# An attention and mixture-of-experts layer on one core: another order of the steps at pass boundaries and in the first pass

## The reference, cut to what matters

```python
q = layernorm(x); k = v = ctx
ig, fg = gates(concat(q, k, v))
cs = cumsum(log_sigmoid(fg))
log_D = where(tril, cs[:, :, None] - cs[:, None, :], -inf) + ig[:, None, :]
D = exp(log_D - max(log_D))
C = (q @ k.T / sqrt(32)) * D
h = (C / (max(|C.sum()|, exp(-max(log_D))) + 1e-6)) @ v
x = x + layernorm(h) * ln_scale
u = layernorm(x)
h_s = sum over 2 shared experts of gelu(rmsnorm(u) @ W1 + b1) @ W2 + b2
h_r = sum over the top 2 of 8 routed experts, weighted by their gates
out = x + u + h_s + h_r
```

## Time and profile before

| what | us |
|---|---|
| median of 3 runs | 1325.37 (1324.14 to 1329.71) |
| the profiled execution's own time | 1325.87 |
| its span, first to last instruction | 1324.1 |
| PE busy | 1160.5 |
| DVE busy | 941.8 |
| ACT busy | 805.9 |
| unit 0 of batch 0 starts | 92.0 |
| pass 0 ends (base sum of batch 0) | 229.9 |
| steady passes | 91.8 to 95.7 each |
| the block of the routed tiles begins | 850 |

### The profile page before, as it was taken

One profiled execution on the slowest core, in us unless ns is written; L12 is line 12 of the kernel. 1 busy time (PEld: TensorE's weight loads), 2 busy tenths in 40 slices (PEclk: granted clock), 3 DMA queues, 4 the chain that ended last, 5 costly groups with the idle time before them and its releaser, 6 DMA issues. The chain is left out here.

```text
span 1324.1 us, 21782 instructions
## 1 busy us (share of the span) xinstructions
PE 1160.5 (88%) x7861; PEld 1016.8 (77%) x7861; DVE 941.8 (71%) x2263; ACT 805.9 (61%) x1392; POOL 348.4 (26%) x319
## 2 busy tenths in 40 slices
PE   2839984898998997997997979799999999999996
PEld 1537763677676775885875867799999999999996
DVE  6765659677686686595694545488888888888883
ACT  3315532554554564453564425399999999999994
POOL 7102132041131221221320202023333333333333
PEclk8859885999998998998998989899999999999998
DMA  5000000110010010010000103578888888888882
GB/s 184 32 17 17 16 33 32 32 64 33 19 47 33 29 37 32 33 33 32 33 17 17 41 1 113 160 228 236 232 219 219 223 234 237 236 226 221 219 223 25
DMA packets 141690, 136.16 MB, mean 103 GB/s; under 512 B 48598, under 2 KB 127584, under 8 KB 141584
## 3 DMA queue, kind: packets, MB, share of 16 engines
q1 hardware_dynamic: 122948, 111.68, 26.7%
q0 software_dynamic: 14304, 18.75, 8.5%
q10 hardware_dynamic: 4332, 4.34, 0.9%
HBM read 109.42 MB, written 25.33 MB: 102 GB/s over the span
## 5 line engine op out<-in xcount | busy, mean ns | idle before, releaser
L1328 DVE TENSOR_TENSOR wlo<-big,whi 128x512 fp32r<-128x512 f32 x312 | 220.1, 717 | 21.5 <-ACT whi L1281 14.3
L569 ACT ACTIVATE shared_hraw<-bank,b1s 128x512 f32<-128x512 f32 x128 | 88.0, 688 | 196.4 <-PE bank L1091 196.2
L1281 ACT CAST whi<-big 128x512 fp32r<-128x512 f32 x312 | 191.1, 615 | 5.4 <-PEq L414 5.1
L1253 PE MATMUL bank<-xhi,whi 128*128 128x256 f32 x624 | 175.7, 282 | 6.7 <-DVE xlo L1342 5.1
L1231 PE MATMUL bank<-whi,hhi 128*128 128x256 f32 x624 | 178.3, 286 | 0.0
L1231 PE MATMUL bank<-whi,hlo 128*128 128x256 f32 x624 | 174.6, 280 | 0.0
L1253 PE MATMUL bank<-xlo,whi 128*128 128x256 f32 x624 | 174.6, 280 | 0.0
L1231 PE MATMUL bank<-wlo,hhi 128*128 128x256 f32 x624 | 174.6, 280 | 0.0
L1253 PE MATMUL bank<-xhi,wlo 128*128 128x256 f32 x624 | 174.6, 280 | 0.0
L1074 PE MATMUL bank<-whs,shared_hhi 128*128 128x256 f32 x512 | 150.0, 293 | 27.4 <-DVE shared_hlo L811 27.4
L811 DVE TENSOR_TENSOR shared_hlo<-shared_hraw,shared_hhi 128x512 fp32r<-128x512 f32 x128 | 89.3, 703 | 117.1 <-ACT shared_hhi L572 115.1
(11 more groups left out here) (274 smaller groups left out, 2691.6 us busy)
## 6 DMA issues: line engine op xcount, KB each, us to landing
big<-in_L_ffn_W_r_dram SPq DMA_DIRECT2D x78, 1024.0 KB, 7.2
qcT<-sorted_tokens SPq DMA_DIRECT2D x39, 260.0 KB, 2.9
xb<-in_x_dram SPq DMA_DIRECT2D x8, 512.0 KB, 4.5
cb<-in_ctx_dram SPq DMA_DIRECT2D x8, 512.0 KB, 3.6
xr<-in_x_dram SPq DMA_DIRECT2D x8, 512.0 KB, 3.6
out_dram<-base ACTq DMA_DIRECT2D x8, 512.0 KB, 2.9
sorted_tokens<-chunk SPq DMA_DIRECT2D x9, 260.0 KB
out_dram<-yt,token POOLq DMA_INDIRECT x78, 4.0
```

Source lines behind the costliest of these rows:

```text
L569: nc.scalar.activation(hraw[:, k % NHB, :], up_bank[k % 2][:, :], ACT.Gelu, bias=b1s[:, k // M, k % M:k % M + 1]).then_inc(gelu_done, 1)
L1253: last = nc.tensor.matmul(ub[:, 0:T], w[i][:, wsl], x_[i][:, k, :], start=k == 0 and t == 0, stop=k == KD - 1 and t == 2)
L1281: nc.scalar.copy(whi[i][:, psl], raw[i][:, psl]).then_inc(t_whi, 1)
L1328: nc.vector.tensor_tensor(wlo[i][:, psl], raw[i][:, psl], whi[i][:, psl].bitcast(fp32), ALU.subtract).then_inc(t_wlo, 1)
```

## The change

Three things change.

The strings: in `START`, which ran only batch 0's `front` and `back`, the eight `g` steps of batch 1 now stand between the last rounds, the normalisation and the first two units of batch 0. `FIRST` opens with `S 0` and has its units between the steps of the attention of batch 1, as `ORDER` has. In all strings `A` (routing) moves behind the first `1`. The query mask of DVE becomes a step `M` of its own behind `G`. The last step of `front` is cut in two on DVE, `C` and `c`, at L715 and L716, and `c` comes behind the last unit of the pass.

The end of a pass: PE's last down projection (`late`, step `L`) moves behind the next pass's states and first scores. `finish` becomes the step `Y` behind `H`. The down banks' first write of a pass waits for `fin_ready`.

The waits and loads: PE's transposes of batch 1 wait for three blocks of batch 0 only, and no more for its logits. The load of batch 1's context moves ahead of the wait for the weight pieces.

```diff
--- before.py
+++ after.py
@@ -347,10 +347,10 @@
 
 
 
-        START = "f f f w w w f f w w f S w w w 0 w w 0 w w 1 w w 1 w 2 w 2 3 3 T T T V V V W h u X u".split()
-        FIRST = "g g U U g U U g U g U U U g U U S 0 U 0 A 1 U 1 Q F 2 U F 2 B P 3 U 3 D G T E T T R V V V R W X C".split()
-        ORDER = "S 0 H 0 U A 1 U F 1 U Q 2 U F 2 B U P 3 U 3 D U G T E U T U Z T U Z R V U V U V U R U W U X C U".split()
-        ORDER_6 = "S 0 H 0 U A 1 U 1 U Q 2 U 2 B U P 3 U 3 D U T E U T T U V U V V U W U X U U U U".split()
+        START = "f f f f w w w f f w w f f S w w w 0 w w 0 w w 1 w w g 1 w 2 w g 2 3 3 g T T T V V g g V W h g u g u X g".split()
+        FIRST = "S 0 U 0 1 A U 1 F U Q 2 U F 2 B U P 3 U 3 D G M T E U T U T R V U V U V U R U W U X C U c".split()
+        ORDER = "S 0 L H Y 0 U 1 A U 1 F U Q 2 U F 2 B U P 3 U 3 D U G M T E U T U Z T U Z R V U V U V U R U W U X C U c".split()
+        ORDER_6 = "S 0 L H Y 0 U 1 A U 1 U Q 2 U 2 B U P 3 U 3 D U T E U T T U V U V V U W U X U U U U".split()
         assert ORDER.count("U") == U and ORDER_6.count("U") == U and FIRST.count("U") + START.count("u") == U and START.count("w") == PIECES
         att_bank, up_bank, down_bank = psum[0:4], psum[4:6], psum[6:8]
 
@@ -377,6 +377,10 @@
                         k += 1
                     elif step == "H":
                         parts["hand_over"](b)
+                    elif step == "L":
+                        parts["late"](b - 1)
+                    elif step == "Y":
+                        parts["finish"](b - 1)
                     elif step == "P":
                         parts["base"](b)
                     elif step in "AQBDE" or step == "Z" and b == B - 1:
@@ -385,7 +389,7 @@
                         next(routes[b])
                     elif step == "d":
                         parts["idle"]()
-                    elif step in "FGRCfg":
+                    elif step in "FGMRCcfg":
                         f = 0 if step == "f" else 1 if step == "g" else b + 2
                         if f < B:
                             if f not in fronts:
@@ -395,8 +399,8 @@
                         if b + 1 not in backs:
                             backs[b + 1] = parts["back"](b + 1)
                         next(backs[b + 1])
-                if b >= 0:
-                    parts["finish"](b)
+            parts["late"](B - 1)
+            parts["finish"](B - 1)
 
         class Steps:
 
@@ -434,14 +438,16 @@
                 load(xb, x_v, 1, s_x)
                 sp.wait_ge(s_wls, 1)
                 sp.dma_start(slots_w[PIECES - 1], w_piece(PIECES - 1)).then_inc(s_wlast, 16)
+                sp.wait_ge(state_done, 1)
+                load(cb, c_v, 1, s_c)
                 sp.wait_ge(s_wls, PIECES - 1)
                 load(xr, x_v, 0, s_xr)
                 for b in range(1, B):
                     if b > 1:
                         sp.wait_ge(q_ready, b)
                         load(xb, x_v, b, s_x)
-                    sp.wait_ge(state_done, b)
-                    load(cb, c_v, b, s_c)
+                        sp.wait_ge(state_done, b)
+                        load(cb, c_v, b, s_c)
                     sp.wait_ge(x1_ready, b)
                     load(xr, x_v, b, s_xr)
                 sp.wait_ge(s_zero, 1)
@@ -521,6 +527,7 @@
                         nc.scalar.copy(qcT[:, :, j * P:(j + 1) * P],
                                        att_bank[j][:, :].rearrange("p (k s) -> p k s", s=P)).then_inc(qcT_ready, 1)
                     yield
+                    yield
                     sc.wait_ge(gates_done, b + 1)
                     if b == 0:
                         sc.wait_ge(s_gate, 16 * GATE_LOADS)
@@ -608,7 +616,7 @@
                     nc.scalar.copy(xhs[:, :, :], unT[:, :, :]).then_inc(xhs_ready, 1)
 
                 passes(sc, {"front": front, "back": back, "unit": unit, "hand_over": hand_over, "split": split, "idle": lambda: None,
-                            "base": lambda b: None, "finish": finish, "route": route})
+                            "base": lambda b: None, "finish": finish, "late": lambda b: None, "route": route})
 
             @block.vector
             def _(dve):
@@ -944,7 +954,7 @@
                     dve.sem_inc(tables_known, 1)
 
                 passes(dve, {"front": front, "back": back, "unit": unit, "hand_over": hand_over, "split": split, "idle": lambda: None,
-                             "base": to_add, "finish": finish, "route": route})
+                             "base": to_add, "finish": finish, "late": lambda b: None, "route": route})
 
             @block.tensor
             def _(pe):
@@ -956,11 +966,10 @@
 
                     pe.wait_ge(q_ready, b + 1)
                     pe.wait_ge(s_c, 16 * b + 16)
-                    if b > 0:
+                    if b == 1:
+                        pe.wait_ge(hn_ready, J - 1)
+                    if b > 1:
                         pe.wait_ge(hn_ready, J * b)
-                    if b == 1:
-                        pe.wait_ge(logit_read, 1)
-                    if b > 1:
                         pe.wait_ge(gT_ready, b - 1)
                     for j in range(J):
                         for k in range(KD):
@@ -1067,6 +1078,8 @@
                 def second(b, k):
 
                     pe.wait_ge(hlo_ready, U * b + k + 1)
+                    if b > 0 and k == 0:
+                        pe.wait_ge(fin_ready, b)
                     e, m = k // M, k % M
                     wsl = slice(WN + m * D, WN + (m + 1) * D)
                     for j in range(J):
@@ -1094,8 +1107,10 @@
                     if k >= LAG:
                         second(b, k - LAG)
                     if k == U - 1:
-                        for late in range(U - LAG, U):
-                            second(b, late)
+                        second(b, U - 2)
+
+                def late(b):
+                    second(b, U - 1)
 
                 def route(b):
                     yield
@@ -1139,7 +1154,7 @@
                     mm(psum[5][:, :], ident[:, :], ident[:, :].unsqueeze(1).to_broadcast([P, HG, P]), start=True, stop=True)
 
                 passes(pe, {"split": lambda n: None, "idle": idle, "front": front, "back": back, "unit": unit, "hand_over": lambda b: None,
-                            "base": lambda b: None, "finish": lambda b: None, "route": route})
+                            "base": lambda b: None, "finish": lambda b: None, "late": late, "route": route})
 
         stage_a.close()
 
```

## The result

| | before | after |
|---|---|---|
| median, us | 1325.36 | 1243.82 (1242.61 to 1245.87) |
| span of the profiled execution, us | 1324.1 | 1242.0 |
| predicted median, us | | 1247 (1228 to 1272) |

The account below looks back on a forecast made before the run. TensorE, busy 88%, was taken as the bound, losing time in waits behind VectorE's order. Gains 40.6 (five intervals), 8.5 (pass 6 to 7) and 35.6 (up to pass 1) sum to 84.7, less 6 for clock: 1247 us, range 1228 to 1272.

Parts of the forecast that it names:

- The boundary: End of a pass: cut exponent block frees the last residual early, down projection fills a wait; unit 0 5.9 us earlier.
- 1 A: Routing put behind the first round 1, so `ct` no longer waits for it on VectorE: 3.0 us a pass.
- Five intervals: From unit 0 of pass 1 to unit 0 of pass 6: 474.4 us become 433.7, a gain of 40.6 us.
- The opening: Batch 1's steps run inside batch 0's start: unit 0 at 93.65 against 91.99, mark behind unit 2 at 121.8.
- Pass 0: From the mark behind unit 2 to unit 0 of pass 1: 80.0 us, so that unit starts 35.6 us earlier.
- The clock: TensorE slow stretches behind short idle pieces at the passes: 6 us taken off the gain, bounds 0 and 12.
- (a): Clock falls as often as now, two more slow stretches in each of seven passes: 24 us less gain, 1271; chance 0.12.
- (e): TensorE gets only the lower clock from each boundary to block 3, slower than before: 1433; chance 0.02.
- (b): Opening slips by late copies or states waiting for GpSimd, unit 2 comes 10 us later: 1257; chance 0.1.
- (d): Boundaries give nothing and only pass 0 shrinks: 1290; chance 0.06.
- (f): Units can't be packed into pass 0, which stays 15 us longer: 1262; chance 0.08.
- (c): Opening: GpSimd and VectorE block one another, normalised tokens (L792) come up to 8 us later: 1255; chance 0.04.

Follow-up runs that it names:

- e5: Changed kernel with the exponent block whole again ahead of the last unit: 1241.93 us, ratio 0.9290.
- e3: Changed kernel with the routing's first step ahead of round 1 again in every pass: 1275.43 us, ratio 0.9571.
- e6: Changed kernel with the cut of the exponent block one instruction later, behind the product that makes the third part: 1245.24 us, ratio 0.9315.
- e7: Changed kernel with VectorE's query masking in passes 1 to 5 moved from beside GpSimd's to behind the gates' steps: 1246.46 us, ratio 0.9328.
- e10: Changed kernel with GpSimd's share of the query masking left out from batch 2 on (comparison only): 1245.23 us, ratio 0.9346.
- e4: Changed kernel with the last unit's second half back inside it and the sum into base back at the pass's end: 1258.51 us, ratio 0.9454.
- e9: Changed kernel with the exponent block whole and VectorE's query masking moved away from GpSimd's in every pass: 1240.32 us, ratio 0.9301.
- e1: Changed kernel with the opening and pass 0 of the kernel before: 1282.02 us, ratio 0.964.
- after_third: Changed kernel itself, run again in a later session: 1249.14 us, ratio 0.9373.

## Why the prediction was right

**The boundary.** Predicted 5.9 us. From L1065 to the next L835 the kernel before took 27.0 us in passes 2 to 5, the changed one 20.62, or 22.2 at every second boundary: 6.4 and 4.8. The chain came as told: the residual at once behind the cast, the eight products as the last release, the late second half under the wait for `ct`. What the account leans on, the cut that lets the residual run early, was not needed, as e5 showed: without it the boundary is 0.97 us shorter. Mis-sized was the second part of the exponent block: 5.3 us by the old row, 4.5 measured (278.02 to 282.54), because it now lies mostly behind GpSimd's work and runs faster there.

**"1 A".** Predicted 3.0 us. From L835 to L1065 68.65 us became 65.58: 3.1. Undone by itself (e3) it cost 3.7 us a pass. The strings also move `F` (the moments of the next queries, on VectorE) behind the second `1`; no run prices that apart.

**Five intervals.** 40.2 measured. The sum before the clock term was 40.6; the block's 0.5 to 0.8 us more and the clock's 1.6 us at two of the boundaries nearly cancel.

**Pass 6 to 7.** 7.4 us for 8.5. The wait of 4.13 us for the token halves is gone from the row at 714.59, but the clock is at 0.50 from 688 to 698 still; what that costs was not measured apart.

**The opening.** Unit 0 of batch 0 at 94.51, predicted 93.65. Two terms were off and cancelled in part. The first: L1065 came at 88.97, not at 86.95, 2.5 us behind the kernel before's 86.45 where 0.5 was predicted. 0.7 of it is there when VectorE has the values of block 3 (70.26 for 69.57). TensorE had started them 0.9 us earlier than before, but they ran at the lower clock (3.73 us, granted clock 0.56 and 0.58 from 66 to 74). The other 1.8 us arise behind them, in VectorE's normalisation of batch 0, beside which GpSimd's mask of batch 1 now runs. Time lines of VectorE and GpSimd in the changed kernel:

```profile
77.08 0.47 DVE L639 SCALAR_TENSOR_TENSOR nw_u<-nw_u 128x4 f32<-128x4 f32 x1
...
78.38 2.47 DVE L649 TENSOR_SCALAR x<-hh,mv_u,nw_u 128x256 f32<-128x256 f32 x4
...
75.32 6.26 POOL L473 TENSOR_SCALAR big<-qcT,headmask 128x512 f32<-128x512 f32 x4
```

and the same four products in the kernel before, with GpSimd idle:

```profile
76.94 1.38 DVE L641 TENSOR_SCALAR x<-hh,mv_u,nw_u 128x256 f32<-128x256 f32 x4
```

The products cost 1.1 us more, and two instructions of 128x4 took 0.57 and 0.47 us for 0.17 and 0.16, 0.7 us more; behind the products both kernels take 8.1 us to the transposes. The prediction put this overlap at nothing, by the earlier trace rows. The second term went the other way: the mask took 1.66 us, not 2.9, since the step was lent from a stretch in which GpSimd was busy. The mark behind unit 2 (the end of the values of batch 1's block 0) was forecast at 118.7 to 124.9 with 121.8 taken; it came at 118.5, the full-clock end: the states ran at the lower clock (106.08 to 110.4), as predicted, and from 110.5 on the granted clock is 0.98.

**Pass 0.** From that mark 84.4 us, predicted 80.0. A steady pass was put at 86.75 and took 86.2, 0.5 less. Two terms failed. The first is the 1.85 us up to block 3: from the mark to the first `hn` of block 3 (149.96) it is 31.5 us, and pass 2 takes 32.0 from unit 0 to the same place, so 0.5 came. TensorE has one up projection fewer there and one down projection more, so its work is the same; 1.85 and 5.66 together are more than the 5.61 us (three up, one down) that the same paragraph counts. The second is the 5.66 less 0.8 us behind block 3: from `hn` to L1065 pass 0 takes 28.7 us and pass 2 31.6, so 2.9 came for 4.9. Of this stretch the part from the mask on takes 24.7 and 25.8 us, 1.1 less, because VectorE's own chain (23.3 of 24.6 us busy) sets it whether TensorE has its units or not; the prediction had that chain's 24.7 us in hand and used it only for the transposes' wait. Another 1.6 us is the slow stretch at 196 to 200. The mark's 3.3 us the other way brought unit 0 of pass 1 to 202.89 for 201.8, so the 34.5 us are right by two errors that offset.

**The clock.** 6 us were put in against the sum of 84.7; the spans differ by 82.1, so 2.6 are missing. In the trace the slow boundaries are three (1.6 us each) and the stretch at 688 to 698; the others in the passes cost nothing, such as that at 360 to 364: the boundary that holds it and the stretch at 370 to 374 takes 22.23 us, and the one with a stretch at 544 to 548 alone 22.17. So the size was about right for what is on the path, and the faster exponent block gave part back.

**Rivals.** (a), the clock falls as often as before, and (e), it never comes back, fall: the slow stretches are fewer, and none is longer than 4 us in a steady pass. (b), (d) and (f) fall with the mark at 118.5, 289.11 - 202.89 = 86.2 and 202.89. (c), one engine blocked by the other, falls in its full size, up to 8 us. But a weaker form of it is true: 1.8 us at L802 itself, and e6, e7 and e10 show it elsewhere. The row chosen against it, could not show it: it was a tensor_tensor of 128x1024, and the forms that slowed most are casts and products with a scalar. That unit 0 came only 0.9 us late in spite of it is luck: the shorter mask gave 1.2 us back in the same stretch.

Of what was named to show it: the passes are 86.2 and 87.8 us; no wait for L821 is left at the boundary, and L1023 waits 1.30 us for L733 (some 2 were named); 0.7 us ahead of the second L1056 instead of 2.24; no 14.8 us in pass 0. Of the signs that were to show it wrong, no steady pass is above 90 us and the granted clock of 230 to 700 is 0.98; one came true, L1065 in the opening at 88.97, later than 88 us. Unit 0 was 0.9 us late by it and the shorter mask together.

## What to carry to other kernels

Of two edits that remove the same wait, test each without the other: here either took 4 to 6 us from a boundary, and one of them on top of the other cost 1 us. And move one thing at a time: the sum that went along with the second half accounts for all of the 0.87 us between e4 and the changed kernel. What counts is which engine's chain ends last in the stretch; here 12 matmuls on the engine that waits could be moved at no price (e4), while 1.27 us put ahead of the chain's last instruction cost 0.87. A duration lent from another place holds only if the same neighbours are busy there; and a row that shows one form of instruction undisturbed says nothing of another form.

## What the runs showed of the hardware

**VectorE's casts and scalar products beside GpSimd.** The cast of 24x512 took 0.41 us alone and 0.76 beside GpSimd's weighted values; four mask products of 128x512 1.66 and 2.9; four products of 128x256 in the opening 1.38 and 2.47; eight products with `negsel` 2.18, and 2.81 where GpSimd worked beside the first 1.1 us of them (e5). A tensor_tensor of 128x1024 took 1.22 us beside GpSimd's mask and 1.23 without, but the residual of 128x512 took 0.69 us alone and 0.99 at 277.10, and 1.06 beside the mask against 0.69 in e10. Of the eleven small instructions of 128x4 beside the mask in the opening two were slowed, to 0.57 and 0.47 us; the others kept 0.16 to 0.20. Over whole instructions VectorE was slowed by 1.3 to 1.9 times, those two small ones by 3. GpSimd gives way too: its four mask products took 6.7 us beside VectorE's and 6.2 without them (e7), and its copy of 128x1024 took 1.04 us in the opening, 1.30 beside the mask products and 1.78 in e7, beside VectorE's tensor_tensor of 128x1024. The Trainium skill, "SBUF — State Buffer", section "SBUF: two separate sides", tells of an exclusive lock, for some of VectorE's forms, under which the loser fully blocks. Here VectorE's four mask products were done in 2.9 us while GpSimd worked through a copy of 1.3 us and went on with a mask of 6.7, so no run here shows VectorE fully blocked. Whether GpSimd was, for the half microsecond of its copy in e7, is open.

**The same idle piece, with either clock behind it.** Ahead of the transposes of pass 0 TensorE was idle for 3.28 to 3.39 us in six traces. In four of them the granted clock stayed at 1.00, in two (e3 and e9) it fell to 0.50 for some 10 us. It was not shown what decides.

**A wait that nobody released.** In the later sessions three engines stood still in pass 0 (but for e1, which has the old pass 0), and ScalarE in the steady passes, with no release in the profile; in e1 to e4 VectorE did so too in some of them. Time lines of ScalarE, TensorE and VectorE in `after_third`:

```profile
240.07 0.69 ACT L577 ACTIVATE shared_hraw<-bank,b1s 128x512 f32<-128x512 f32 x1 [1.58 <-remote]
...
152.89 0.41 PE L976 MATMUL bank<-ident,qn 128*128 128x128 f32 x2 [2.60 <-issue]
...
151.45 0.43 DVE L761 TENSOR_TENSOR hn<-bank,eexp 128x264 f32<-128x264 f32 x1 [3.13 <-remote]
```

The trace of the changed kernel from the first session has none of these. L835 to L1065 takes 67.0 us with them and 65.6 without, and pass 0 2.4 us more. It goes with the session and not with the kernel, since the kernel before is 7 to 12 us slower in those sessions too. The profile also lists loads of instructions by DMA. In `after_third` two of them fall into 239 to 240 us, just ahead of ScalarE's restart at 240.07; in the first session's trace they come at 236 and 238 us and nobody stands still. Late instructions may be the cause; no run tests it, and it stays open.
